# A two-layer audio tower: experts run on gathered rows in a pipeline stage of their own

## The reference

```
h = dct(frames)                                    # 626 x 128 per item
h = h + mamba_two_directions(layernorm(h))         # "attn" of layer 0
h = h + experts(layernorm(h))                      # 8 experts, 2 per row
h = h + local_attention(layernorm(h))              # window of 8 frames
h = h + three_top_k_layers(layernorm(h))           # k = 64 of 512, 128 of 256, 64 of 512

def experts(x):                                    # per row x, all 8 experts
    p = softmax(x @ gate_w + gate_b)               # 8 weights
    keep the two largest of p, zero the rest
    h = gelu(x @ w1[e] + b1[e])                    # 128 -> 512
    y[e] = h @ w2[e] + b2[e]                       # 512 -> 128
    return sum over e of p[e] * y[e]
```

## Time and profile before

| | us |
|---|---|
| median of three runs | 8677.74 (8659.9 to 8679.93) |
| the profiled execution | 8673.34 |
| its span, first to last instruction | 8670.7 |
| DVE busy | 7915.2 (91%) |
| PE busy | 6907.8 (80%) |
| ACT busy | 3389.3 (39%) |
| POOL busy | 2524.6 (29%) |
| bytes moved | 128.48 MB, 15 GB/s |

### The profile page before, as it was taken

How to read it: one execution, slowest core, us unless ns; L and a number is a source line. 1 busy time by engine, 2 the same in 40 slices (tenths; PEclk the granted TensorE clock), 3 DMA queues, 4 the chain that set the end, 5 groups by cost and what they waited for, 6 DMA issues and landing times.

```text
span 8670.7 us, 114685 instructions
## 1 busy us (share of the span) xinstructions
PE 6907.8 (80%) x35336; PEld 5042.4 (58%) x35336; DVE 7915.2 (91%) x23276; ACT 3389.3 (39%) x5803; POOL 2524.6 (29%) x2481
## 2 busy tenths in 40 slices
PE   6788887788878788878788887888878888777863
PEld 4566565566655565655565655566655656555642
DVE  2699999999999999999999999999999999999998
ACT  2344433344433344433344433444333444333431
POOL 1332123332133332233322233321233322333320
PEclk8788877788877788877888877888877888777875
DMA  1000000000000000000000000000000000000000
GB/s 57 15 17 15 8 12 17 17 17 15 7 13 17 17 16 14 10 13 17 17 15 10 10 17 17 17 15 8 12 17 17 17 15 7 13 17 17 14 2 3
DMA packets 95339, 128.48 MB, mean 15 GB/s; under 512 B 7600, under 2 KB 94096, under 8 KB 94096
## 3 DMA queue, kind: packets, MB, share of 16 engines
q1 hardware_dynamic: 94736, 120.71, 5.0%
HBM read 109.68 MB, written 11.01 MB: 14 GB/s over the span
## 4 chain that ended last, share of the span: by engine, by line
DVE 55%; PE 32%; issue 5%; POOL 4%; ACT 3%; DMA 1%; DVEq 0%; SPq 0%; POOLq 0%; ACTq 0%
DVE m L1038 17%; DVE work L1040 15%; PE pM L585 9%; PE pM L574 7%; DVE a L1040 4%; DVE ab L904 3%; PE pS L507 2%; DVE hid L992 2%; ACT hid L778 2%; DVE h L982 2%; PE pS L473 2%; DVE stats L863 2%; PE pS L501 2%; DVE a L1049 2%; PE pS L527 1%
## 5 line engine op out<-in xcount | busy, mean ns | idle before, releaser
L1040 DVE MATCH_REPLACE8 work<-m,work 128x256 f32<-128x256 f32 (+1 forms) x4192 | 2156.0, 522 | 0.0
L1038 DVE MAX8 m<-work 128x8 f32<-128x256 f32 (+1 forms) x4192 | 2014.0, 526 | 1.0
L574 PE MATMUL pM<-uT,cst 128*128 128x320 f32 x4096 | 1473.2, 480 | 179.5 <-DVE h L973 117.3
L311 POOL TENSOR_TENSOR rstd<-vare,mhalf 128x5 f32<-128x5 f32 x160 | 187.5, 1172 | 4671.2 <-DVE vare L869 4671.1
L778 ACT ACTIVATE hid<-pM,cst 128x320 f32<-128x320 f32 x2048 | 1061.6, 528 | 1031.2 <-PE pM L574 685.8
L585 PEld LDWEIGHTS pM<-cst,hid 128*128 128x128 f32 x10240 | 1191.9, 193 | 184.6 <-DVE h L982 110.8
L585 PE MATMUL pM<-cst,hid 128*128 128x128 f32 x10240 | 1219.2, 277 | 97.9 <-DVE h L982 97.2
L574 PEld LDWEIGHTS pM<-uT,cst 128*128 128x128 f32 x4096 | 690.5, 199 | 758.5 <-ACT hid L778 533.2
L473 PE MATMUL pS<-u_fm,wconv_s 128*128 128x315 f32 (+1 forms) x3072 | 861.3, 432 | 0.0
L507 PE MATMUL pS<-Mt,Xw 121*64 121x121 f32 x3072 | 377.9, 392 | 492.1 <-DVE Mt L915 492.1
L473 PEld LDWEIGHTS pS<-u_fm,wconv_s 128*128 128x128 f32 (+1 forms) x3072 | 496.1, 167 | 347.5 <-issue 92.9
(11 more groups left out here) (195 smaller groups left out, 11986.4 us busy)
## 6 DMA issues: line engine op xcount, KB each, us to landing
ab<-decay_rows SPq DMA_DIRECT2D x384, 230.7 KB
x_sb<-in_x SPq DMA_DIRECT2D x32, 256.0 KB
out<-hk SPq DMA_DIRECT2D x32, 256.0 KB
cst<-in_weights SPq DMA_DIRECT2D x2, 2048.0 KB, 12.0
hid<-in_setup SPq DMA_DIRECT2D x1, 1904.0 KB, 20.9
out<-hk SPq DMA_DIRECT2D x32, 57.0 KB
x_sb<-in_x SPq DMA_DIRECT2D x32, 56.5 KB
cst<-in_weights SPq DMA_DIRECT2D x1, 1344.0 KB, 17.0
```

The costliest lines, as they stand in the source:

```text
L574: nc.tensor.matmul(pM[:, 512 * (n % 2):512 * (n % 2) + W // 2], w1[:, e, j * P:(j + 1) * P], uT[:, lo:lo + W // 2], start=True, stop=True) ...
L1038: link(nc.vector.max(m[i], now[i]), len(tiles) - 1)
L1040: link(nc.vector.match_replace(work[i], m[i], now[i], GONE), len(tiles) - 1 if r or firsts is None else 0)
```

## The change

The pipeline gets a fourth stage: stage 2 is the experts, stage 3 the attention, stage 4 the top-k layers. Every engine has a new string of digits, SP too, and an item is now four iterations under way.

The experts run only on rows that were sent to them. After the gate, PE counts with two triangular and full matrices of ones how many rows before each row chose the same expert (L666, L669), and DVE turns that into a slot number for each of the two choices of a row, and an expert number for each of 17 tiles (MT = 2 * 5 + 7) of 128 slots. Ten indirect DMAs from POOL, each for 128 rows, scatter the normalised rows to `routed_rows` in memory. SP reads them back four tiles at a time, and for every tile 592 KB of weights (128 x 1156 words) of the tile's expert into a ring of three. PE turns the tile, multiplies it up (four products of 128 x 128) and down (one for the bias, four of 128 x 128); ACT does four Gelus and a copy. SP writes the answers to `answer_rows`, ten more indirect DMAs on POOL gather them, and DVE adds them in ten instructions.

```diff
-BATCHES = E * TILES // 4
 KB = 4
+MT = 2 * TILES + E - 1
+GROUPS = (MT + 3) // 4
+PAIRS = (MT + 1) // 2
+WR = 3
+EC = 4 * P + KB * P + KB + P
+WHOLE = 2.0 ** 23
+STAGE_LAG = (0, 1, 2, 3)
...
-PE_ORDER = ("33333322112222222222223223223222231221232322222322332222231211122222222222222222222221313232232322223232"
...
+PE_ORDER = ("14444413333232413111121111111111111111111111114211211121111111111111141111111121111111111111211111411111"
...
+SP_ORDER = ("1122111311111132222222222222222222222222244")
...
+        def sp_stage1(sp, b):
+            sp.wait_ge(G["xT_ps"].s, G["xT_ps"](b, 0))
+            xb = x_d[bass.ds(b, 1), :, :]
+            sp.dma_start(x_sb[:, 0:4, :], xb[:, 0:4 * P, :].rearrange("o (t p) d -> p (o t) d", p=P)).then_inc(G["x_in"].s, 16)
+            sp.dma_start(x_sb[0:REAL - 4 * P, 4, :], xb[:, 4 * P:REAL, :].rearrange("o p d -> p (o d)")).then_inc(G["x_in"].s, 16)
+            yield
+            sp.wait_ge(G["dA_sb"].s, G["dA_sb"](b, 1))
+            sp.wait_ge(G["scanned"].s, G["scanned"](b, 0))
+            sp.dma_start(rows_d.rearrange("k (h t) -> (k h) t", h=NH), dAT[:]).then_inc(G["dA_out"].s, 16)
+            yield
+            sp.wait_ge(G["dA_out"].s, G["dA_out"](b, 16))
+            for k in range(2 * CH):
+                ch, d = divmod(k, 2)
+                at = d * CH + ch
...
+        def sp_stage2(sp, b):
+            sp.wait_ge(weights_in, 64)
+            sp.wait_ge(G["tiles_done"].s, G["tiles_done"](b, 1))
+            which = expert_of_tiles(sp)
+            def weights(i):
+                sp.wait_ge(G["tile_done"].s, G["tile_done"](b, max(i + 1 - WR, 0)))
+                sp.dma_start(expert[i % WR][:], experts_d[bass.ds(which[i], 1), :, :].rearrange("o p c -> p (o c)")).then_inc(G[f"expert{i % WR}"].s, 16)
+            def routed(g):
+                n = min(4, MT - 4 * g)
+                if g >= 2:
+                    sp.wait_ge(G["tile_done"].s, G["tile_done"](b, 4 * (g - 2) + 2))
+                sp.dma_start(rows[:, g % 2 * 4:g % 2 * 4 + n, :],
+                             routed_d[4 * g * P:(4 * g + n) * P, :].rearrange("(t p) d -> p t d", p=P)).then_inc(G[f"rows{g % 2}"].s, 16)
+            def answers(p):
+                n = tiles_of(p)
+                sp.wait_ge(G["kept"].s, G["kept"](b, 2 * p + n))
+                sp.dma_start(answers_d[2 * p * P:(2 * p + n) * P, :].rearrange("(t p) d -> p t d", p=P),
+                             turned[:, 2 * p % 4:2 * p % 4 + n, 0, :]).then_inc(G[f"y_out{p % 2}"].s, 16)
+            for i in range(WR):
+                weights(i)
+            yield
+            sp.wait_ge(scattered.s, scattered(b, 160))
+            sp.wait_ge(G["moe_done"].s, G["moe_done"](b, 0))
+            routed(0)
+            routed(1)
+            for i in range(MT):
+                if i + WR < MT:
+                    yield
+                    weights(i + WR)
+                if i % 4 == 1 and i // 4 + 2 < GROUPS:
+                    yield
+                    routed(i // 4 + 2)
+                if i % 2 == 1 or i == MT - 1:
+                    yield
+                    answers(i // 2)
+        def sp_stage4(sp, b):
+            sp.wait_ge(G["out_sb"].s, G["out_sb"](b, TILES))
+            o = out_d[bass.ds(b, 1), :, :]
+            sp.dma_start(o[:, 0:4 * P, :].rearrange("o (t p) d -> p (o t) d", p=P), hk[:, 0:4, :]).then_inc(G["out_dma"].s, 16)
+            sp.dma_start(o[:, 4 * P:L, :].rearrange("o p d -> p (o d)"), hk[0:L - 4 * P, 4, :]).then_inc(G["out_dma"].s, 16)
+            yield
...
         def pool_stage2(pool, b):
+            normalized(pool, 1, 1, b, un, h2).then_inc(G["u2_done"].s, 1)
+            yield
+            pool.wait_ge(G["u2_done"].s, G["u2_done"](b, 1))
+            pool.wait_ge(G["slots_done"].s, G["slots_done"](b, 1))
+            nc.gpsimd.tensor_tensor(ticks[:, 0:1], zero1[:, 0, :], zero1[:, 0, :], ALU.add)
+            for k in range(2 * TILES):
+                nc.gpsimd.indirect_dma_start(routed_d, bass.IndirectOffsetOnAxis(ap=slot[:, k:k + 1], axis=0), un[:, k % TILES, :], None,
+                                             bounds_check=MT * P - 1, oob_is_err=False).then_inc(scattered.s, 16)
+            yield
+            pool.wait_ge(G["y_out0"].s, G["y_out0"](b, 80))
+            pool.wait_ge(G["y_out1"].s, G["y_out1"](b, 64))
+            nc.gpsimd.tensor_tensor(ticks[:, 1:2], zero1[:, 0, :], zero1[:, 0, :], ALU.add)
+            for k in range(2 * TILES):
+                nc.gpsimd.indirect_dma_start(rows[:, k, :], None, answers_d, bass.IndirectOffsetOnAxis(ap=slot[:, k:k + 1], axis=0),
+                                             bounds_check=MT * P - 1, oob_is_err=False).then_inc(gathered.s, 16)
...
+            def turn(i):
+                if i % 4 == 0:
+                    arrived = G[f"rows{i // 4 % 2}"]
+                    pe.wait_ge(arrived.s, arrived(b, 16 * (i // 8 + 1)))
+                return nc.tensor.transpose(pM[:, bank(i) + P:bank(i) + 2 * P], rows[:, i % 8, :], ident)
+            def up(i):
+                yield
+                landed = G[f"expert{i % WR}"]
+                pe.wait_ge(landed.s, landed(b, 16 * (i // WR + 1)))
+                if i < 2:
+                    pe.wait_ge(G["turned_sb"].s, G["turned_sb"](b, i + 1))
+                else:
+                    pe.wait_ge(G["kept"].s, G["kept"](b, i - 1))
+                for j in range(KB):
+                    last = nc.tensor.matmul(pM[:, bank(i) + j * P:bank(i) + (j + 1) * P], w1_of(i, j), turned[:, (i + 2) % 4, 1, :],
+                                            start=True, stop=True)
+                last.then_inc(G["hid_ps"].s, 1)
+            def down(i):
+                yield
+                pe.wait_ge(G["hid_sb"].s, G["hid_sb"](b, i + 1))
+                at = pM[:, bank(i):bank(i) + P]
+                nc.tensor.matmul(at, c("ones", 1), b2_of(i), start=True, stop=False)
+                for j in range(KB):
+                    last = nc.tensor.matmul(at, hid[:, i % 2, j, :], w2_of(i, j), start=False, stop=(j == KB - 1))
+                if i + 2 < MT:
+                    last = turn(i + 2)
+                last.then_inc(G["tile_done"].s, 1)
...
+            def gelu(i):
+                yield
+                act.wait_ge(G["hid_ps"].s, G["hid_ps"](b, i + 1))
+                if i >= 2:
+                    act.wait_ge(G["tile_done"].s, G["tile_done"](b, i - 1))
+                for j in range(KB):
+                    at = i % 2 * 512 + j * P
+                    last = nc.scalar.activation(hid[:, i % 2, j, :], pM[:, at:at + P], ACT.Gelu, bias=b1_of(i, j))
+                last.then_inc(G["hid_sb"].s, 1)
...
+            dve.wait_ge(G["rank_ps"].s, G["rank_ps"](b, 1))
+            ranks = pM[:, RANKS:RANKS + (TILES + 1) * E].rearrange("p (t e) -> p t e", e=E)
+            link(nc.vector.tensor_scalar(tally[:, 0, :], ranks[:, TILES, :], 1.0 / P, (P - 1) / (2.0 * P), ALU.mult, ALU.add))
...
+            nc.vector.tensor_scalar(tile_e[:], tile_f[:], float(E - 1), None, ALU.min).then_inc(G["tiles_done"].s, 1)
...
+            nc.vector.tensor_copy(slot[:], slot_f[:].rearrange("p j t -> p (j t)")).then_inc(G["slots_done"].s, 1)
+            yield
+            dve.wait_ge(gathered.s, gathered(b, 160))
             dve.wait_ge(G["h3_kept"].s, G["h3_kept"](b, 0))
-            nc.vector.tensor_tensor(h2[:].rearrange("p t d -> p (t d)"), h[:].rearrange("p t d -> p (t d)"), pM[:, 0:W],
-                                    ALU.add).then_inc(G["acc_done"].s, 1)
-            for i in range(BATCHES):
-                yield
-                dve.wait_ge(G["exp_ps"].s, G["exp_ps"](b, i + 1))
-                dve.wait_ge(G["acc_done"].s, G["acc_done"](b, i + 1))
-                for m in range(4 * i, 4 * i + 4):
-                    e, t = divmod(m, TILES)
-                    last = nc.vector.scalar_tensor_tensor(h2[:, t, :], pM[:, B2 + P * (m % 4):B2 + P * (m % 4 + 1)], gate[:, t, e:e + 1],
-                                                          h2[:, t, :], ALU.mult, ALU.add)
-                last.then_inc(G["acc_done"].s, 1)
-            yield
-            dve.wait_ge(G["acc_done"].s, G["acc_done"](b, BATCHES + 1))
-            moments(link, 1, h2, G["var2"])
+            dve.wait_ge(G["u4_done"].s, G["u4_done"](b, 0))
+            for t in range(TILES):
+                last = nc.vector.scalar_tensor_tensor(h3[:, t, :], rows[:, t, :], top8[:, t, 0:1], h2[:, t, :], ALU.mult, ALU.add)
+            link(last)
+            for t in range(TILES):
+                last = nc.vector.scalar_tensor_tensor(h3[:, t, :], rows[:, TILES + t, :], top8[:, t, 1:2], h3[:, t, :], ALU.mult, ALU.add)
+            last.then_inc(G["moe_done"].s, 1)
```

More of the change, by code:

```diff
@@ new lines, in run @@
+        def run(engine, order, *stages):
+            last = max(STAGE_LAG)
+            for i in range(last):
+                merged(order, *[stage(engine, i - lag) if i >= lag else None for stage, lag in zip(stages, STAGE_LAG)])
+            with engine.Fori(last, NB) as b:
```

(3 more changed lines are left out.)

397 lines of the change are left out of this document (213 added, 184 removed).

## The result

The changed kernel takes 8725.16 us (median of 7 runs, 8711.08 to 8735.79) against 8677.74. The ratio is 1.0056, with a 95% interval from 1.0044 to 1.0068: slower by half a per cent. The forecast was 8740.

What follows compares the result with a forecast made beforehand. DVE was taken as the bound: 235.4 us of work plus 27.0 of waits make a period of 262.4; head 511, 29 periods 7610, tail 615 and 4 more give 8740 us, with an own range of 8640 to 8870.

Steps and rivals of the forecast that it cites:

- DVE's work: DVE's busy time per iteration: 247.3 us less 7.1 of instructions and 4.8 of scans, giving 235.4.
- The scans: DVE's scans, no longer beside POOL's attention steps: 12 chunks save up to 0.41 us each, 4.8 in all.
- The decays' wait: DVE's first scan waits behind SP's register reads and loads of weights and rows: stall 8.5 us an iteration.
- S + 25.5: S is the end of the slots, 2.9 us behind L895's place; the first `ab` lands 25.5 us later.
- the tiles' work: PE and ACT get 17 tiles, about 4 us each with about 8 us available: hidden, counted 0.
- rival B: Stall hidden, waits at the start and for the decays down about 10.4 us: period 252, 8440 us; chance 0.30.
- The start: Start of an iteration: x loads behind the previous item's store, DVE idles 8.0 us, replacing 9.05 of old waits.
- one of its own signs of being wrong: The forecast is wrong if, among other signs, the x load does not hold PE's transposes at an iteration's start.
- The other waits: DVE's smaller waits: 6.3 us for attention, gate's exp, dt, links and colder PE, plus 4.2 old small ones.
- Rival C: PE becomes cold in the 12 chunks, costing 12 us: period 274.4, 9084 us; chance 0.16.
- Rival D: An indirect DMA holds POOL 2.3 us or more; rows and broadcasts 7 us later: period 269.4, 8939; chance 0.12.
- Head and tail: The fourth stage adds a short iteration at each end: head 511 us, tail 615.

Runs made afterwards that it cites:

- experiment 12: Changed kernel with 20 additional POOL additions of two 128x640 operands an item behind the scatters, on their own buffer: 8865.39 us.
- Experiment 1: Changed kernel with SP issuing the four broadcasts of the decays ahead of register reads, weights and rows: 8867.92 us.
- experiment 8: Changed kernel, SP's broadcasts first, PE's two turns behind the first two chunks' products and first up product behind the third's: 8454.52 us.
- experiment 9: Changed kernel with the loop body written out twice: 8680.15 us.
- experiment 7: Changed kernel, SP's broadcasts first, PE's two first turns and first up product 16 to 20 projection products later: 8672.77 us.
- experiment 5: Changed kernel with one scatter and one gather an item instead of ten each, outputs wrong: 8693.26 us.
- experiments 2 and 6: 2: changed kernel, SP's register reads and weights before the decays, rows last, 8843.19 us; 6: 2 with one scatter and gather an item, 8631.67 us.

## Why the prediction was right, step by step

**DVE's work: 235.4 forecast, 237.5 measured.** The scans did what was said (-0.45 each, 5.3 in sum, forecast 4.8); experiment 12 shows why. What the step left out is that POOL's attention goes on somewhere. It now stands beside L1247, which was not slowed before:

```profile
L1247 DVE SCALAR_TENSOR_TENSOR a<-work,a 128x256 f32<-128x256 f32 x48 | 44.2, 921 | 0.0
```
```profile
L1078 DVE SCALAR_TENSOR_TENSOR a<-work,a 128x256 f32<-128x256 f32 x45 | 18.8, 417 | 0.3
```

The second row is the same instruction in the kernel before. Five an item at 0.50 more are 2.5 us, which is about the whole of the miss. That POOL causes it is read from the times: over 25 iterations the 50 of these instructions that ran beside no work of POOL took 0.42 us, 25 beside its L481 took 1.63, and 50 beside its L510 1.09. One of them:

```profile
3038.99 1.62 DVE L1247 SCALAR_TENSOR_TENSOR a<-work,a 128x256 f32<-128x256 f32 x1
```

No run tested it.

**The decays' wait: 8.5 forecast, 9.0 measured.** The place, the mechanism and the size are right, but not the parts. Of S + 25.5, measured S + 25.7 (34.3 to 60.0), the decays took 8.7 us where I had 11.8; the reads 5.8 where I had 3; from the issue of the broadcasts to the scan 7.5; and the 3.7 between are issues. The loads of rows are not slow in themselves. I took 118 GB/s from the earlier trace rows; all transfers together moved 329 GB/s with the engines at 0.97. That rate was one of a single store, over a stretch in which the DMA engines were busy for 0.41 only. The Trainium skill (DMA: Bandwidth & Descriptors, Specifications), by which 512 bytes are enough for line rate, was nearer than my reading of the rate. At 329 GB/s the rows take 1.6 us, 2.8 less than my 4.4; but the four broadcasts are 0.95 MB themselves, 2.9 us at that rate, and the sum has hardly room for them: its listed terms, 11.8 + 3 + 4.1 + 4.4, leave 2.2 of the 25.5 for all issues and the broadcasts. So two pairs of errors of about 3 us cancelled: the place of the wait was foreseen, its size was in part luck.

The step also saw DVE's wait only. PE's wait for the rows was not priced at all (of the tiles' work it says "so it is hidden"), and rival B, "the stall is hidden", was priced as if the broadcasts decided alone. Experiment 1 shows that they do not, and 8 that with both chains gone the period is 252.76, where rival B had 252.

**The start: 8.0 forecast, 8.5 measured, by another chain.** It was to be x behind the store. It is POOL's L409 and L518 for 4.6, then the jump for 3.9. x lands 6.7 us after the issue of the store (measured in experiment 9) and not 8.2; in the changed kernel that is, by estimate, 2.2 us before PE came back. Only experiment 9, which takes every second jump away, makes it the wait. The prediction named this as one of its own signs of being wrong ("if the x load does not hold the transposes"). The mechanism of this term is wrong, then, and that its number fits is luck.

**The other waits: 10.5 forecast (6.3 and 4.2), 6.2 measured.** This is the largest miss in the sum. The work came 2.1 us above the forecast, the two named waits together 1.0 above, and these 4.3 below: that is how 262.4 and 261.1 come so close.

**Rival C, the low clock.** In the changed kernel it did not come true: the stretch of the chunks had 1.00, and the pitch was 1.97. The mechanism is real and strong, though. The clock did fall to the lower level around PE's wait for the rows, but it was back before the chunks began. In experiment 7, where the pause stands right ahead of them, it reached into the chunks.

**Rival D and the indirect DMAs.** POOL is held for 1.27 us each, next to the assumed 1.2, and experiment 5 shows them hidden in the period. A scatter lands 2.2 us after its issue; that agrees with the Trainium skill's fit for a DMA from GpSimd (same page, Anatomy of one DMA), an estimate of 2.15 for 64 KB, and shows that this is latency and not POOL's time. What I did not foresee is that the scatters slow SP (experiments 2 and 6). It stays without effect in the changed kernel, where SP reads at 43.6 and later, at full speed even beside the last scatters.

**Head and tail.** 1126 forecast, 1141.3 measured, the head 24.5 above. Of these 15.5 are the indirect DMAs, scatters and gathers together (experiment 5). The tail is 9 below, the loop 39 below, and the median lies 13 above the span where I had 4: 24.5 - 9 - 39 + 9 is 15 less than the forecast 8740.

So the change does give what it promises, 9.4 us of DVE an iteration, and loses 8.5 to waits and, by the extra ramp, about 77 us in all ((535.5 + 605.8) against 142 + 233 + 427 + 262.3). With the broadcasts, the two turns and the first up product in other places, and not one instruction less, it is 2.5% faster than the kernel before (experiment 8), and 3.1% with the loop's body written twice.

## What to carry to other kernels

Behind one in-order queue, look for every consumer of what stands in it, not only the one that waits now. Here DVE and PE waited for the same SP queue, and freeing one made the kernel slower (8868). When an engine near the bound pauses for data, move the step that pauses behind work that is ready: besides the pause itself, the low clock after it goes. And a DVE instruction that POOL's work slows has to be counted wherever that work goes: here 5.3 us came off the scans, and 2.5 came back at L1247.
